# Two-tile attention units: queries, values, reciprocals and late transposes in another order

## Chip, cores and metric
The kernel runs on one core of a Trainium2 chip. The metric is the device time of one execution in microseconds (us); lower is better.

## What is computed
Four cross-attention layers in a row over x of shape (8, 256, 256), with one context ctx of shape (8, 64, 256) as keys and values; all in fp32. The change is within layers 0 and 2. Their core is, for each of the 8 batch rows:

```python
q = (layernorm(x) @ q_w + q_b)          # layer 0: x itself, context normalised
k, v = ctx @ k_w + k_b, ctx @ v_w + v_b  # 16 heads of 16
attn = softmax(where(mask, q k^T / 4, min))   # 256 x 64 per head
x = x + (attn v) @ w_o + bias            # layer 0: tanh(gate) * (...)
```

Layer 1 is the same with 32 heads of 8 and a layer norm after the sum. Layer 2 goes on with an MLP of 1024, and layer 3 is two attentions with heads of 128 and another MLP.

## The kernel before, in words
Five engines run their own instruction lists; semaphores tie them. Layers 0 to 2 are 24 units, one for each layer and batch row (`UNITS`, units 0 to 7, 8 to 15, 16 to 23; `NU` = 24). A unit of layer 0 or 2 has two tiles of 128 queries by 16 heads by 64 keys, one of layer 1 has four. Tiles are numbered through (`FIRST[u]` is the first of unit u).

The work is a pipeline over the units. In turn u TensorE makes the scores of unit u (`masks` L553, then `both_scores` L566 in two turns 0 and 1, two banks `sc`), the transposes of the last tile of unit u-1 (`late_tiles`, `probs_transposed` L588), the values of unit u+1 (`values` L477, bank work[3]), the source transposes of unit u+2 from unit 8 on (`source` L499, bank work[2]), the transposes of the softmax reciprocals of unit u-1 (`reciprocals_transposed` L597), the weighted values of u-1 (`weighted` L613, bank work[2]), the transposes of the first tile of unit u (banks work[0], work[1]), the queries of unit u+1 (`queries` L515, bank work[3]) and the output product of u-1 (`output` L633). A unit without a source product runs all but that.

VectorE reduces the maximum of each tile (L1112) and subtracts it (L1128), ScalarE takes the exponential (`exponentials`, L1631) and copies each result out of its bank: the transposed tile (`probs_out`, L1638), values (L1602), queries (L1567 and L1570), source, reciprocals (`reciprocals_out`, L1655). GpSimd adds the exponentials in halves and quarters (L1948, L1951), VectorE finishes the sum (L1134) and takes the reciprocal (L1141), and GpSimd spreads it over the head's columns (L1938); those go to TensorE to be transposed. VectorE's list has `unit_residual(u-2)`, the late tile's sum, `unit_reciprocals(u-1)` and only then the maximum of unit u's first tile. In layer 0's unit 5 VectorE also splits a bias in parts (`bias_parted`, L1168). In unit 17 ScalarE's `ln_finish` (L1616) and GpSimd's `norm_affine` (L1968) finish layer 1's last row. Layer 1's units have an order of their own in the same loops (`len(tiles) == 4`), and unit 16 too (`len(late) == 2`).

Of the kernel before, what the change touches and what calls it, by code (L numbers as in the profile page):

```python
# [98 lines left out]
def build(nc, A, out):  # L99
    with ExitStack() as ctx:  # L100
# [248 lines left out]
        def spread_done(u):  # L349
# [3 lines left out]
            return (a_spr, n) if u + 1 < NU and UNITS[u + 1][0] == 1 else (p_spr, u + 1 - n)  # L353

        def mlp_bank(b):

            return work[3] if b == 0 else work[2 + b % 2]
# [82 lines left out]
        def tensor(e):  # L440
# [74 lines left out]
            def queries(u):  # L515
                layer, _ = UNITS[u]
                w = w_small[f"l{layer}_wq"]
                e.wait_ge(s_in[f"l{layer}_wq"], 16)
                if u < B:
                    e.wait_ge(s_in["xT0" if u < 2 else "xT1"], 16)  # L520
                    src = xT[:, u, :, :]
                else:
                    e.wait_ge(a_sT, u - B + 1)
                    src = srcT[u % 3]


                if u > 0:
                    e.wait_ge(a_vd, u + 1)
                if u < 2 or 1 not in (UNITS[u - 1][0], UNITS[u - 2][0]):
                    e.wait_ge(a_rT, u - 1)  # L530
                if UNITS[u] == (1, 6):
                    e.wait_ge(a_key, 6)
                for o in range(DC):
                    for c in range(DC):
                        last = mm(work[3][:, o * T:(o + 1) * T], w[:, c, o * P:(o + 1) * P], src[:, c, :],  # L535
                                  start=(c == 0), stop=(c == DC - 1))
                last.then_inc(pe_q, 1)
# [50 lines left out]
            def probs_transposed(k):  # L588
                e.wait_ge(a_exp, k + 1)
                for half in range(2):  # L590
                    e.wait_ge(a_pT, 2 * (k - 1) + half + 1)
# [5 lines left out]
            def reciprocals_transposed(u):  # L597

                e.wait_ge(*spread_done(u))

                e.wait_ge(a_vd, min(u + 3, NU))
                e.wait_ge(a_qT, min(u + 2, NU))
                if u + 1 < NU and 1 in (UNITS[u][0], UNITS[u + 1][0]):
                    e.wait_ge(a_qT, u + 3)
                if u == NU - 1:
                    e.wait_ge(d_mT, 2)
                for c in range(DC):
                    for t in range(TT):
                        last = tr(work[3][:, c * T + t * P:c * T + (t + 1) * P], spread[u % 2][:, t, c * P:(c + 1) * P],
                                  ident[:, :])  # L610
                last.then_inc(pe_rT, 1)
# [58 lines left out]
            def mlp_source(b):  # L670
                e.wait_ge(*NORMS["m2", b])
                if b == 0:

                    e.wait_ge(a_rT, NU - 1)
                elif b == 1:
                    e.wait_ge(a_rT, NU)
                elif b == 2:
                    e.wait_ge(d_res, NU)
                else:
                    e.wait_ge(d_mT, 2 * (b - 2) + 2)  # L680
# [18 lines left out]
            def projected(b):  # L699
# [4 lines left out]
                if b < 2:  # L704
                    e.wait_ge(a_pT, 2 * NK)
                else:
                    e.wait_ge(d_mr, b - 1)
# [17 lines left out]
            for u in range(NU + 1):  # L725
# [35 lines left out]
                else:  # L761
                    if u + 1 < NU:
                        values(u + 1)
                        both_scores(u, 1)
                    if B <= u + 2 < NU:
                        source(u + 2)
                    for k in late:
                        probs_transposed(k)
                    if u == NU - 1:
                        both_scores(u, 1)  # L770
                    if u == NU:
                        hidden(0, 0)
                    if u > 0:
                        reciprocals_transposed(u - 1)
                        weighted(u - 1)
                    if u == NU:
                        hidden(0, 1)
                if tiles:
                    probs_transposed(tiles[0])
                if u + 1 < NU and len(late) < 2:  # L780
                    queries(u + 1)
                if u == NU - 1:
# [760 lines left out]
        def scalar(e):  # L1543
# [108 lines left out]
            def reciprocals_out(u):  # L1652
                e.wait_ge(pe_rT, u + 1)
                e.wait_ge(d_o, u - 1)
                act(recT_bufs[u % 2], work[3][:, :], ACT.Copy).then_inc(a_rT, 1)  # L1655

# [31 lines left out]
            for u in range(NU + 1):  # L1688
# [31 lines left out]
                if len(late) == 2:  # L1720
# [4 lines left out]
                    unit_source(u + 2)  # L1725
                    unit_queries(u + 1)
                else:
                    if u + 1 < NU:
                        unit_values(u + 1)
                    if B <= u + 2 < NU:  # L1730
                        unit_source(u + 2)
                    if u == NU:
                        mlp_source_high(0)
                    for k in late:
                        probs_out(k)
                    if tiles:
                        exponentials(tiles[0])
                if u > 0:
                    reciprocals_out(u - 1)
                if ended[0] == 1:  # L1740
                    ln_finish(("l1", ended[1]), xb(ended[1]), xb(ended[1]))
                if tiles:
                    probs_out(tiles[0])
                    exponentials(tiles[1])
                if u + 1 < NU and len(late) < 2:
                    unit_queries(u + 1)
                if u + 2 < NU and UNITS[u + 2][0] == 1:
# [425 lines left out]
```

## Time and profile before

| | us |
|---|---|
| median of 3 runs | 1095.81 |
| lowest, highest | 1095.37, 1098.17 |
| the profiled execution | 1095.92 |
| its span | 1094.0 |
| TensorE busy | 1008.7 (92%) |
| VectorE, ScalarE, GpSimd busy | 650.5, 512.8, 401.1 |

The span runs from the first to the last instruction. PE is TensorE, DVE VectorE, ACT ScalarE, POOL GpSimd. The chain of work that ended last lies on PE for 78% of the span, on ACT for 8%, POOL 5%, DVE 4%. The units of layers 0 to 2 end at about 368 us; the rest is the two MLPs and layer 3.

### The profile page before, as it was taken

The numbers are of one execution on the slowest core, as the hardware profiler recorded it, in microseconds if no ns is written. First come the engines' busy times: TensorE is split into PE (matmuls) and PEld (weight loads), VectorE is DVE, ScalarE is ACT, GpSimd is POOL, SyncE is SP. The second block draws the span as 40 slices with busy tenths as digits, with TensorE's granted clock in tenths as the row PEclk, the third lists the DMA queues.
The fourth block names the chain that finished last, engine by engine and source line by source line (L and its number), as shares of the span: only waits on it lengthen the run. The fifth ranks groups of instructions, "written<-read, shape, count | busy, mean of one in ns | idle before, by whom it ended". The sixth has DMA issues, their size and how long they took to land.

```text
span 1094.0 us, 18102 instructions
## 1 busy us (share of the span) xinstructions
PE 1008.7 (92%) x7252; PEld 794.6 (73%) x7252; DVE 650.5 (59%) x1119; ACT 512.8 (47%) x1026; POOL 401.1 (37%) x424
## 2 busy tenths in 40 slices
PE   5988888888789799899999999999999999989997
PEld 3656555545566699887777777777777777759997
DVE  4558887787678568735444555775345444465552
ACT  2446776675677545434323332333233323345542
POOL 2433578768976433201112212321122122253110
PEclk9999998999999999999999999999999999999999
DMA  9102000000000150020000022310000000200000
GB/s 329 44 2 78 1 1 1 1 1 1 1 2 1 44 208 1 1 78 1 1 1 1 1 75 81 116 39 1 1 1 1 1 1 1 77 1 11 20 20 30
DMA packets 17463, 34.90 MB, mean 32 GB/s; under 512 B 3554, under 2 KB 8420, under 8 KB 16740
## 3 DMA queue, kind: packets, MB, share of 16 engines
q1 hardware_dynamic: 17380, 33.75, 8.9%
q8 instruction: 57, 0.93, 0.3%
q14 instruction: 26, 0.21, 0.1%
HBM read 31.65 MB, written 2.10 MB: 31 GB/s over the span
## 4 chain that ended last, share of the span: by engine, by line
PE 78%; ACT 8%; POOL 5%; DVE 4%; issue 3%; DMA 0%; SPq 0%; POOLq 0%; ACTq 0%; DVEq 0%
PE work L928 11%; PE work L805 10%; PE scores L864 10%; PE work L881 5%; PE work L917 4%; PE work L593 3%; PE work L535 3%; PE work L645 3%; PE work L666 3%; PE work L667 3%; PE work L668 3%; PE scores L666 3%; PE scores L668 3%; PE scores L667 3%; PE work L447 2%
## 5 line engine op out<-in xcount | busy, mean ns | idle before, releaser
L928 PE MATMUL work<-pair,probsT 128*128 128x256 f32 x512 | 118.8, 385 | 11.1 <-ACT pair L1821 8.9
L1907 POOL TENSOR_SCALAR stat<-stat 128x2 f32<-128x2 f32 (+1 forms) x49 | 11.1, 227 | 298.8 <-DVE stat L1050 297.4
L928 PEld LDWEIGHTS work<-pair,probsT 128*128 128x128 f32 x512 | 94.6, 190 | 34.9 <-issue 20.4
L805 PE MATMUL work<-ctxT,w 128*128 128x128 f32 x992 | 116.1, 275 | 1.8 <-ACT pair L1821 1.1
L805 PEld LDWEIGHTS work<-ctxT,w 128*128 128x128 f32 x992 | 114.5, 192 | 3.0 <-ACT pair L1821 1.3
L864 PE MATMUL scores<-pair,act_bufs 128*128 128x512 f32 x256 | 115.2, 593 | 0.0
L1812 ACT ACTIVATE pair<-work 128x512 f32<-128x512 f32 x64 | 38.2, 597 | 160.3 <-PE work L881 160.3
L1802 ACT ACTIVATE kvT<-work,cols 128x128 f32<-128x128 f32 x120 | 34.2, 368 | 142.2 <-PE work L805 142.2
L2061 POOL TENSOR_TENSOR probs<-probs,smax 128x1024 f32<-128x1024 f32 x22 | 42.0, 1908 | 150.9 <-DVE smax L1439 150.9
L1419 DVE TENSOR_REDUCE smax<-scores 128x16 f32<-128x1024 f32 x32 | 39.2, 1224 | 79.6 <-PE scores L864 79.6
L864 PEld LDWEIGHTS scores<-pair,act_bufs 128*128 128x128 f32 x256 | 46.3, 190 | 46.0 <-issue 45.9
L881 PEld LDWEIGHTS work<-kvT,w 128*128 128x128 f32 x512 | 61.9, 192 | 15.3 <-issue 15.3
L1410 DVE TENSOR_TENSOR kvT<-work,cols 128x512 f32<-128x512 f32 x32 | 22.1, 691 | 83.8 <-PE work L805 83.8
L1112 DVE TENSOR_REDUCE smax<-scores 128x16 f32<-128x1024 f32 x48 | 58.3, 1214 | 16.7 <-PE scores L581 16.2
L881 PE MATMUL work<-kvT,w 128*128 128x128 f32 x512 | 62.4, 275 | 1.8 <-issue 1.8
L917 PE MATMUL work<-w,kvT 128*64 128x256 f32 x512 | 62.3, 385 | 0.0
L593 PE MATMUL work<-ident,pair 128*128 128x128 f32 x256 | 36.7, 289 | 24.9 <-ACT w L1638 12.9
L593 PEld LDWEIGHTS work<-ident,pair 128*128 128x128 f32 x256 | 29.4, 147 | 41.3 <-ACT pair L1631 36.1
L1948 POOL TENSOR_TENSOR pair<-pair 128x512 f32<-128x512 f32 x32 | 41.2, 1289 | 32.8 <-ACT pair L1631 32.2
L1960 POOL TENSOR_TENSOR x<-x,rows_late 128x512 f32<-128x512 f32 x32 | 47.8, 1497 | 10.3 <-DVE act_bufs L1056 8.6
L1638 ACT ACTIVATE w<-work 128x512 f32<-128x512 f32 x88 | 47.5, 592 | 8.2 <-PE work L593 8.1
L1948 POOL TENSOR_TENSOR pair<-probs 128x512 f32<-128x512 f32 x32 | 40.9, 1277 | 27.9 <-ACT probs L1631 27.7
(190 smaller groups left out, 2577.0 us busy)
## 6 DMA issues: line engine op xcount, KB each, us to landing
w<-in_l_wk SPq DMA_DIRECT2D x8, 512.0 KB, 6.1
w<-in_l_wq SPq DMA_DIRECT2D x8, 512.0 KB, 6.7
w<-in_l_wo SPq DMA_DIRECT2D x8, 512.0 KB, 7.6
w<-in_l_wv SPq DMA_DIRECT2D x8, 512.0 KB, 5.2
x<-in_x SPq DMA_DIRECT2D x1, 2048.0 KB, 13.0
out<-x SPq DMA_DIRECT2D x8, 256.0 KB, 2.1
pair<-in_xT SPq DMA_DIRECT2D x1, 1536.0 KB, 7.3
pair<-in_l_fc SPq DMA_DIRECT2D x1, 1024.0 KB, 4.9
```

Of the source, the lines that this page charges most:

```text
L593: last = tr(work[half][:, q * P:(q + 1) * P], probs[k % 4][:, (4 * half + q) * P:(4 * half + q + 1) * P], ident[:, :])
L666: mm(bank, s_hi, m_hi, start=start, stop=False)
L667: mm(bank, s_hi, m_lo, start=False, stop=False)
L668: return mm(bank, s_lo, m_hi, start=False, stop=stop)
L805: last = mm(bank[:, h * P:(h + 1) * P], w[:, c, (4 * g + h) * K3:(4 * g + h + 1) * K3], ctxT[:, c, p * P:(p + 1) * P], start=(c == 0), sto ...
L864: last = mm(sc[j % 2][:, half * BANK:(half + 1) * BANK], fixed[j // 2 % 2][:, c, t * P:(t + 1) * P], pk[n % 2][:, bb, c, half * BANK:(half ...
L881: last = mm(step_banks(j)[2 + c][:, h * P:(h + 1) * P], w3_wq[:, 4 * g + h, c * P:(c + 1) * P], kvT[i % 2][:, h, :], start=True, stop=True)
L917: last = mm(bank[h * S:(h + 1) * S, bb * D:(bb + 1) * D], kvT[2][:, 2 * q + h, bb * S:(bb + 1) * S], w3_wo[:, 4 * g + 2 * q + h, :], start ...
L928: last = mm(step_banks(j + 1)[0][:, 0:D], probsT_bufs[j % 2][:, q, :], pv[n % 2][:, bb, q, :], start=(q == 0), stop=(q == GH // 2 - 1))
L1112: v.tensor_reduce(smax[k % 2][:, 0:GH], s3, X, ALU.max).then_inc(d_max, 1)
L1948: g.tensor_tensor(halves, e3[:, :, 0:n], e3[:, :, n:S], ALU.add).then_inc(p_half, 1)
L1960: g.tensor_tensor(xb(b), xb(b), row(name).unsqueeze(1).broadcast_to([P, TT, D]), ALU.add).then_inc(done, 1)
```

## The change
In the turns of two-tile units, other than unit 16's, TensorE's list is reordered. Before: scores turn 0, values, scores turn 1, source, late tile's transposes, reciprocals' transposes, weighted values, first tile's transposes, queries, output. After: scores turn 0, late tile's transposes, scores turn 1, source, reciprocals' transposes, values, weighted values, queries, first tile's transposes, output. ScalarE's list follows: late tile's copies, source, reciprocals, values, first exponential, queries, (normalisation), first tile's copies, second exponential. Before it was values, source, late tile's copies, first exponential, reciprocals, (normalisation), first tile's copies, second exponential, queries. Between two-tile units the reciprocals' transposes write work[0] (`reciprocals_bank`), whose next use waits for their copy. In unit 0 the values stay ahead of the second turn. The waits are those that the new banks and order need. The lists of VectorE, GpSimd and the DMA queue stay.

```diff
+        def in_pairs(u):
+            return u > 0 and UNITS[u - 1][0] != 1 and (u == NU or UNITS[u][0] != 1)
+        def reciprocals_bank(u):
+            return work[0] if in_pairs(u + 1) else work[3]
@@ queries
                 if u > 0:
                     e.wait_ge(a_vd, u + 1)
-                if u < 2 or 1 not in (UNITS[u - 1][0], UNITS[u - 2][0]):
-                    e.wait_ge(a_rT, u - 1)
@@ probs_transposed
                 e.wait_ge(a_exp, k + 1)
+                u = UNIT_OF[k]
+                if k == FIRST[u] and in_pairs(u):
+                    e.wait_ge(a_rT, u)
@@ reciprocals_transposed
                 e.wait_ge(*spread_done(u))
-                e.wait_ge(a_vd, min(u + 3, NU))
-                e.wait_ge(a_qT, min(u + 2, NU))
-                if u + 1 < NU and 1 in (UNITS[u][0], UNITS[u + 1][0]):
+                if in_pairs(u + 1):
+                    e.wait_ge(a_pT, 2 * FIRST[u + 1] - 1)
+                else:
+                    e.wait_ge(a_vd, u + 3)
                     e.wait_ge(a_qT, u + 3)
@@ TensorE, two-tile units
-                    if u + 1 < NU:
+                    for k in late:
+                        probs_transposed(k)
+                    if u == 0:
                         values(u + 1)
+                    if tiles:
                         both_scores(u, 1)
                     if B <= u + 2 < NU:
                         source(u + 2)
-                    for k in late:
-                        probs_transposed(k)
-                    if u == NU - 1:
-                        both_scores(u, 1)
                     if u == NU:
                         hidden(0, 0)
                     if u > 0:
                         reciprocals_transposed(u - 1)
+                        if u + 1 < NU:
+                            values(u + 1)
                         weighted(u - 1)
                     if u == NU:
                         hidden(0, 1)
+                    if u + 1 < NU:
+                        queries(u + 1)
                 if tiles:
                     probs_transposed(tiles[0])
-                if u + 1 < NU and len(late) < 2:
-                    queries(u + 1)
@@ ScalarE
-                act(recT_bufs[u % 2], work[3][:, :], ACT.Copy).then_inc(a_rT, 1)
+                act(recT_bufs[u % 2], reciprocals_bank(u)[:, :], ACT.Copy).then_inc(a_rT, 1)
@@ ScalarE, two-tile units
+                    reciprocals_out(u - 1)
+                else:
                     if u == NU:
                         mlp_source_high(0)
                     for k in late:
                         probs_out(k)
+                    if B <= u + 2 < NU:
+                        unit_source(u + 2)
+                    if u > 0:
+                        reciprocals_out(u - 1)
+                    if u + 1 < NU:
+                        unit_values(u + 1)
                     if tiles:
                         exponentials(tiles[0])
-                if u > 0:
-                    reciprocals_out(u - 1)
+                    if u + 1 < NU:
+                        unit_queries(u + 1)
                 if ended[0] == 1:
                     ln_finish(("l1", ended[1]), xb(ended[1]), xb(ended[1]))
                 if tiles:
                     probs_out(tiles[0])
                     exponentials(tiles[1])
-                if u + 1 < NU and len(late) < 2:
-                    unit_queries(u + 1)
```

The first sources of the MLP and its projections wait for other counts of the same copies (`mlp_source`, `projected`).

## Rows read from the trace of the kernel before

**Rows 1.** Windows, stages of two-tile units: length, busy per engine, clock, DMA, GB/s
```profile
18.20:113.20 95.00, 82.51 (x754) 57.92 (x752) 59.55 (x77) 51.30 (x94) 40.88 (x48) 0.98 0.20 69
...
267.20:368.30 101.10, 87.15 (x814) 64.20 (x815) 72.17 (x123) 67.19 (x125) 76.33 (x103) 0.97 0.01 1
```

**Rows 2.** Timeline, TensorE, unit 4: start, busy, line, out<-in, count, idle before
```profile
62.43 0.61 PE L562 MATMUL scores<-mask_l,ones_bf 64*128 64x512 bf16 x4
62.96 0.73 PE L581 MATMUL scores<-w,pair 32*128 32x128 f32 x16
63.62 1.08 PE L495 MATMUL work<-w,pair 128*64 128x256 f32 x8
64.63 0.73 PE L581 MATMUL scores<-w,pair 32*128 32x128 f32 x16
65.29 1.09 PE L593 MATMUL work<-ident,pair 128*128 128x128 f32 x8
66.22 0.60 PE L609 MATMUL work<-ident,pair 128*128 128x128 f32 x4
67.12 1.07 PE L629 MATMUL work<-w,pair 128*32 128x256 f32 x16 [0.30 <-ACT w L1638]
69.02 1.09 PE L593 MATMUL work<-ident,probs 128*128 128x128 f32 x8 [0.83 <-ACT probs L1631]
69.95 1.89 PE L535 MATMUL work<-pair,w 128*128 128x256 f32 x8
71.68 1.89 PE L645 MATMUL work<-w,pair 128*128 128x256 f32 x8
```

**Rows 3.** Timeline of the other engines, around the start of unit 4
```profile
60.34 1.06 ACT L1631 ACTIVATE pair<-pair 128x1024 f32<-128x1024 f32 x1 [0.61 <-DVE pair L1128]
...
65.98 1.08 ACT L1638 ACTIVATE w<-work 128x512 f32<-128x512 f32 x2 [0.61 <-PE work L593]
...
63.65 0.42 DVE L1134 TENSOR_REDUCE sums<-pair 128x16 f32<-128x256 f32 x1 [0.36 <-POOL pair L1951]
64.10 0.35 DVE L1141 RECIPROCAL recs<-sums 128x32 f32<-128x32 f32 x1
65.39 1.22 DVE L1112 TENSOR_REDUCE smax<-scores 128x16 f32<-128x1024 f32 x1 [0.94 <-PE scores L581]
...
61.53 1.27 POOL L1948 TENSOR_TENSOR pair<-pair 128x512 f32<-128x512 f32 x1 [1.40 <-ACT pair L1631]
62.89 0.73 POOL L1951 TENSOR_TENSOR pair<-pair 128x256 f32<-128x256 f32 x1
...
64.52 0.61 POOL L1938 COPY pair<-recs 128x512 f32<-128x512 f32 x1 [0.33 <-DVE recs L1141]
```

**Rows 4.** Timeline, the start (units 0 and 1) and unit 5 on VectorE
```profile
25.75 3.31 PE L535 MATMUL work<-pair,w 128*128 128x256 f32 x8
...
33.00 0.60 PE L609 MATMUL work<-ident,pair 128*128 128x128 f32 x4
...
30.66 0.61 POOL L1938 COPY pair<-recs 128x512 f32<-128x512 f32 x1 [0.34 <-DVE recs L1141]
...
88.10 0.90 DVE L1175 CAST bias_parts<-pair 1x256 bf16<-1x256 f32 x3
```

**Rows 5.** Timeline, layer 2: turns 17, 18, 23 (TensorE), 17 and 19 (the others)
```profile
293.76 0.65 PE L609 MATMUL work<-ident,pair 128*128 128x128 f32 x4 [2.06 <-POOL pair L1938]
...
305.40 0.66 PE L609 MATMUL work<-ident,pair 128*128 128x128 f32 x4 [0.84 <-POOL pair L1938]
...
363.57 1.62 PE L593 MATMUL work<-ident,pair 128*128 128x128 f32 x8 [2.07 <-ACT pair L1631]
...
295.62 1.08 ACT L1620 ACTIVATE x<-x,stat 128x256 f32<-128x256 f32 x2
...
322.79 0.82 ACT L1570 ACTIVATE pair<-work,cols 128x256 f32<-128x256 f32 x2
...
297.45 1.27 POOL L1970 TENSOR_TENSOR x<-x,pair 128x512 f32<-128x512 f32 x1
```

More of the change, by code:

```diff
@@ L599, in reciprocals_transposed @@
                 e.wait_ge(*spread_done(u))
-                e.wait_ge(a_vd, min(u + 3, NU))
-                e.wait_ge(a_qT, min(u + 2, NU))
-                if u + 1 < NU and 1 in (UNITS[u][0], UNITS[u + 1][0]):
+                if in_pairs(u + 1):
+                    e.wait_ge(a_pT, 2 * FIRST[u + 1] - 1)
+                else:
+                    e.wait_ge(a_vd, u + 3)
                     e.wait_ge(a_qT, u + 3)
-                if u == NU - 1:
-                    e.wait_ge(d_mT, 2)
                 for c in range(DC):
                     for t in range(TT):
-                        last = tr(work[3][:, c * T + t * P:c * T + (t + 1) * P], spread[u % 2][:, t, c * P:(c + 1) * P],
+                        last = tr(reciprocals_bank(u)[:, c * T + t * P:c * T + (t + 1) * P], spread[u % 2][:, t, c * P:(c + 1) * P],
                                   ident[:, :])
@@ L672, in mlp_source @@
                 if b == 0:
-                    e.wait_ge(a_rT, NU - 1)
-                elif b == 1:
-                    e.wait_ge(a_rT, NU)
+                    e.wait_ge(a_qT, NU)
                 elif b == 2:
                     e.wait_ge(d_res, NU)
+                elif b == 1:
+                    e.wait_ge(d_mT, 2)
                 else:
@@ L705, in projected @@
                     e.wait_ge(a_pT, 2 * NK)
+                    e.wait_ge(a_rT, NU)
                 else:
@@ L766, in tensor @@
                         source(u + 2)
-                    for k in late:
-                        probs_transposed(k)
-                    if u == NU - 1:
-                        both_scores(u, 1)
                     if u == NU:
@@ L1726, in scalar @@
                     unit_queries(u + 1)
+                    reciprocals_out(u - 1)
                 else:
[L1728 to L1731, printed above, removed]
                     if u == NU:
```

## Prediction
> **What bounds the kernel now.** I read the busy times by stage first. The two stages of two-tile units hold 95.0 us (eight units of layer 0) and 101.1 us (the handover from layer 1 and eight units of layer 2); TensorE is busy for 82.5 and 87.2 us of them at a granted clock of 0.98 and 0.97, so some 26 us of gaps are the most that the change can touch [rows 1]. The stages before, between and after keep their order. Then I read TensorE's timeline of one steady unit [rows 2]. Its scores start at 62.43 and the next unit's 11.07 later (each start moves by that from unit to unit). Only two waits stand in it: 0.30 us before the weighted values (L629) and 0.83 us before the first tile's transposes (L593), both for ScalarE. The loop through the second is: scores, maximum and subtraction (VectorE), exponential (ScalarE), transposes, queries, output, the next scores. Last I read the other engines between two units, because the change moves work across that wait [rows 3]. There runs a second loop, hidden now: last exponential of the unit (60.34), two partial sums on GpSimd (61.53, 62.89), sum and reciprocal on VectorE (63.65, 64.10), spread on GpSimd (64.52, ends 65.13), then the reciprocals' transposes (L609). TensorE comes to those only at 66.22, so 1.04 us of slack hides that chain.
>
> **The change, part by part.** (a) The queries (1.73 us from start to start) go ahead of the first tile's transposes, and the late tile's transposes and then the reciprocals' transposes go ahead of the values. The work is the same, TensorE has 9.9 us of it in a unit. If nothing were late, the 1.13 us would go from every unit. (b) On ScalarE the copy of the queries goes ahead of the copies of the first tile's transposes and of the second tile's exponential. (c) The values now wait in TensorE's queue behind the reciprocals' transposes, and the weighted values, the queries, the first tile's transposes and the output behind them. (d) The bank is another (work0 instead of work3): the added wait is for half a tile's copy, long done; I cost it at nothing, it is hidden by (c), and at most the 0.5 us of one copy if it weren't. No DMA and no arithmetic is added; SP's queue is not moved.
>
> What is late next is the second loop. I put the start of the reciprocals' transposes at R. Transposes 0.58, values 1.01, weighted values 1.00, queries 1.73 [rows 2]: the first tile's transposes start at R+4.32 (its exponential is done by R+3.3). ScalarE starts to copy them 0.69 after their start (65.29 to 65.98), two copies take 1.0, so the second exponential starts at R+6.02. From its start to a usable spread it is 60.34 to 65.13 and a hop of 0.05: 4.84 [rows 3]. The period is 6.02 + 4.84 = 10.86 us against 11.07. TensorE would reach the reciprocals 2.8 us into a unit and waits there until 3.8: a 1.0 us wait takes the place of 1.13. A steady unit of layer 0 gains 0.2 us, not 1.1. In layer 2 the copy of the queries is 0.82 instead of 0.58 us [rows 5], so 11.1: no gain, and 0.03 lost.
>
> (e) Start. The first spread ends at 31.27, while TensorE gets to it at 33.00, behind queries that ran slowly after a gap, 3.31 instead of 1.89 us [rows 4, 2]. Now the queries fill that gap: gain 1.7. Three units at 0.2 make it 2.3. At the fifth, the keys of layer 1 on TensorE cover the spread, so its stalls really go, 1.1 more; but behind it VectorE's bias parts (from 88.10, 4.6 us in all) hold the next unit, and start when the first tile's sum is in, 2.7 us earlier [rows 4]. From there 10.9 against some 11.5 us for the last unit: I get 3.0 us of lead at the first four-tile unit. Layer 1 waits for data only, so it should hand the lead on.
>
> (f) Turns 17 and 18, the first of layer 2 in the new order. At 293.76 TensorE has already waited 2.06 us for the spread, which GpSimd and VectorE set, not TensorE [rows 5]. That moment doesn't move, but 1.01 us of values now come after it. Worse, ScalarE's normalisation for layer 1 (at 295.62) stood behind the reciprocals' copy and now stands behind the queries' copy, which ends near 299.0; GpSimd's two affine steps (from 297.45, 1.3 us each) wait for it at the head of its queue, and behind them stand a variance step and the partial sums of the next unit. Step by step: normalised 300.1, affine 302.8, variance 304.4, partial sums 306.5, sum and reciprocal 307.3, spread 308.0 against 305.40 now: 2.6 us lost. 0.3 of it comes back by the next unit, the steady ones lose 0.1 more, and the last unit, whose maximum now waits for the reciprocals, loses 0.4: layer 2 loses 3.0.
>
> (g) TensorE's clock. At 363.57, after 2.07 us of gap, eight transposes took 1.62 us instead of 1.09 (I read that as time at the lower of the clock's two levels, 1.2 GHz), and at 25.75 the queries took 3.31; at 293.76, after 2.06 us, nothing slowed [rows 5, 4]. An episode costs about 1.5 us (3.31 - 1.89 = 1.4 on the queries alone). The change makes a gap of about 3.1 us ahead of 293.76 (0.9 and 2.06 lay apart before, with transposes between), which I take to cost 1.4, and splits the gap before 363.57 into two of 1.3, which I take to save 1.5.
>
> The sum: -3.0 + 3.0 + 1.4 - 1.5 = -0.1 us. The profiled execution took 1095.92 (span 1094.0, 1.9 around it), 0.1 above the median of 1095.81. The sum gives 1095.8 on it; the small errors (0.1 in a period, some eleven times) lean neither way, and I round to 1096.0.
>
> The Trainium skill, "Perfetto Trace Analysis", Identifying the Most-Contended Engine, says to optimise the engine with the highest occupancy first. TensorE is that engine by the rows and its waits are what the change goes for; taken so, the gain would be rival 1's. The same page's section Matmul Optimizations says that the engine scales its power with utilisation and matmuls should come back to back; the slowed rows at 25.75 and 363.57 agree, and it speaks against a change that collects gaps in one place (rival 2).
>
> **Rivals.**
> 1. TensorE becomes the bound, because the spread isn't late. Then 14 units lose 1.13 us and the start 1.7: 17.5, giving 1078. Against it: the chain of 4.84 us is measured, and none of its links is shortened. It would need the second exponential 1.0 us earlier than I have it. Chance 0.07.
> 2. Slower by TensorE's clock: the wait before the reciprocals' transposes of turn 1 (2.0 us by my working) and those of turns 17 and 18 (3.1 and 1.9) each end in the lower level, and the one near 363.57 isn't avoided: -3.0 + 3.0 + 3 x 1.5 = +4.5, giving 1100.4. For it: gaps of 2.07 did it. Against: 2.06 didn't. It decides from a second episode on. Chance 0.18.
> 3. Layer 1 doesn't hand on the lead (its units are set by GpSimd, VectorE and ScalarE in turn, and ScalarE's lead is only 2.4): up to +3.0 on my sum, 1099. Chance 0.1.
> 4. The first units of layer 2 don't lose, because GpSimd catches up: -3.0 - 1.5 and a rest of +0.5, giving 1092. For it: GpSimd has free time in later units. Against: its queue is full from 284 to 305. Chance 0.14.
> 5. The change does nothing: the order is as written but every wait reappears in place. 1095.8. Against: the start's queries have nothing to wait for. Chance 0.03.
> My forecast: 0.48.
>
> **How the numbers follow.** A measurement of this kernel can tell about 0.3% (3.3 us) from no change. Faster by more (under 1092.5): rival 1, most of rival 4 and a tail of the forecast, 0.25. Slower by more (over 1099.1): most of rival 2, half of rival 3 and a tail of the forecast, 0.24. Same: 0.51. The forecast's own range is 1092.5 to 1099.5; with rivals 2 to 4 it is 1090.5 to 1100.8, which leaves out rival 1 and the far ends of the others.
>
> **What would show it.** Right: a wait of about 1.0 us for GpSimd before L609's counterpart in every steady unit, none before the first tile's transposes, a period of 10.9 us in layer 0 and 11.1 in layer 2; the scores of the first four-tile unit 3 us earlier; GpSimd's affine step of the last layer-1 unit after the queries' copy; the reciprocals' transposes of turn 18 at least 2.6 us later, counted from the scores of turn 17. Wrong: periods near 9.9, or no wait for GpSimd. The prediction fails most easily at the clock, whose episodes I can only bound, and at the handover.

## The result, and the profile after

The changed kernel takes 1105.81 us (median of 4 runs, 1104.33 to 1108.47) against 1096.99 us for the kernel before beside it (1095.37 to 1099.27): a ratio of 1.0087, interval 1.0067 to 1.0107. It is slower by 9 us. The forecast of no change, 1096.0 with a range to 1100.8, was wrong. The profiled execution of the changed kernel has a span of 1104.0 us, 10.0 more than before. Ratios go by the fast executions alone, which leaves out one of all those below, of `layer1_filled`: 1485.48 us at a mean granted clock of 0.655.

Where the 10.0 us are, read from the starts of each turn's scores in TensorE's timeline (turn 16's first to turn 17's first, and so on; "first product" is that of the MLP):

| stretch, us | before | after | difference |
|---|---|---|---|
| start to the first scores | 18.2 | 17.8 | -0.4 |
| turns 0 to 7 | 95.0 | 93.6 | -1.4 |
| turns 8 to 15 (layer 1) | 154.0 | 155.5 | +1.5 |
| turn 16 | 19.3 | 19.6 | +0.3 |
| turns 17 and 18 | 26.2 | 34.1 | +7.9 |
| turns 19 to 22 | 44.3 | 45.2 | +0.9 |
| turn 23 to the first product | 13.0 | 12.6 | -0.3 |
| the rest | 724.1 | 725.7 | +1.6 |

The steady turns went as forecast. TensorE's timeline of turn 4 of the changed kernel (start, busy, line, out<-in, count, idle time before it and who ended it), the counterpart of [rows 2]:

```profile
59.98 0.61 PE L566 MATMUL scores<-mask_l,ones_bf 64*128 64x512 bf16 x4
60.51 0.73 PE L585 MATMUL scores<-w,pair 32*128 32x128 f32 x16
61.17 1.09 PE L601 MATMUL work<-ident,pair 128*128 128x128 f32 x8
62.19 0.73 PE L585 MATMUL scores<-w,pair 32*128 32x128 f32 x16
63.80 0.66 PE L617 MATMUL work<-ident,pair 128*128 128x128 f32 x4 [0.88 <-POOL pair L1949]
64.38 1.08 PE L502 MATMUL work<-w,pair 128*64 128x256 f32 x8
65.40 1.07 PE L637 MATMUL work<-w,pair 128*32 128x256 f32 x16
66.40 1.99 PE L539 MATMUL work<-pair,w 128*128 128x256 f32 x8
68.23 1.04 PE L601 MATMUL work<-ident,probs 128*128 128x128 f32 x8
69.10 1.89 PE L653 MATMUL work<-w,pair 128*128 128x256 f32 x8
```

The waits for ScalarE before the weighted values (L637) and before the first tile's transposes (L601) are gone. In their place stands one of 0.88 us before the reciprocals' transposes (L617), for GpSimd's spread. Turns 2 and 3 take 10.95 us from scores to scores (49.03 to 59.98), against 11.07. Turn 4 holds the keys of layer 1 as well: its next scores come 16.36 us later, before 16.48 (62.43 to 78.91). The other engines around the start of the turn before it, the counterpart of [rows 3]:

```profile
47.98 1.07 ACT L1641 ACTIVATE probs<-probs 128x1024 f32<-128x1024 f32 x1
...
51.31 0.42 DVE L1144 TENSOR_REDUCE sums<-pair 128x16 f32<-128x256 f32 x1 [1.42 <-POOL pair L1962]
51.76 0.35 DVE L1151 RECIPROCAL recs<-sums 128x32 f32<-128x32 f32 x1
52.03 1.20 DVE L1122 TENSOR_REDUCE smax<-scores 128x16 f32<-128x1024 f32 x1
...
49.19 1.27 POOL L1959 TENSOR_TENSOR pair<-probs 128x512 f32<-128x512 f32 x1 [1.77 <-ACT probs L1641]
50.54 0.74 POOL L1962 TENSOR_TENSOR pair<-pair 128x256 f32<-128x256 f32 x1
...
52.18 0.61 POOL L1949 COPY pair<-recs 128x512 f32<-128x512 f32 x1 [0.33 <-DVE recs L1151]
```

The chain is the same as before, link by link: exponential 47.98, partial sums 49.19 and 50.54, sum 51.31, reciprocal 51.76, spread from 52.18 to 52.79. TensorE takes it up at 52.85 now; before, it came 1.09 us after the spread's end. VectorE's next maximum stands behind the reciprocal in the same list and isn't held up by it: it starts at 52.03, just behind the end of its scores (51.24 and 0.73).

The large loss is in turns 17 and 18. TensorE, ScalarE and GpSimd there:

```profile
293.74 1.12 PE L617 MATMUL work<-ident,pair 128*128 128x128 f32 x4 [2.92 <-POOL pair L1949]
294.79 1.98 PE L502 MATMUL work<-w,ctxT 128*64 128x256 f32 x8
296.69 1.94 PE L637 MATMUL work<-w,pair 128*32 128x256 f32 x16
298.56 2.36 PE L539 MATMUL work<-act_bufs,w 128*128 128x256 f32 x8
...
308.47 0.63 PE L454 MATMUL work<-ident,act_bufs 128*128 128x128 f32 x4 [1.98 <-ACT act_bufs L1630]
310.79 1.12 PE L617 MATMUL work<-ident,pair 128*128 128x128 f32 x4 [1.70 <-POOL pair L1949]
311.84 1.98 PE L502 MATMUL work<-w,ctxT 128*64 128x256 f32 x8
...
301.68 1.09 ACT L1630 ACTIVATE x<-x,stat 128x256 f32<-128x256 f32 x2
...
302.85 1.27 POOL L1981 TENSOR_TENSOR x<-x,pair 128x512 f32<-128x512 f32 x1 [2.24 <-ACT x L1630]
```

TensorE stands still for 2.92 us before 293.74, and the values and weighted values that follow take 1.98 and 1.94 us instead of 1.08 and 1.07; the same again after 310.79, where gaps of 1.98 and 1.70 us lie ahead. In the windows over the two stretches the last column but two is the granted clock: 0.50, the lower of the two levels (1.2 GHz of 2.4), in both.

```profile
293.70:297.00 3.30, 3.26 (x16) 1.69 (x20) 2.41 (x6) 0.79 (x2) 1.22 (x1) 0.50 0.00 0
310.70:314.00 3.30, 3.21 (x16) 1.70 (x20) 3.27 (x7) 0.75 (x3) 1.26 (x2) 0.50 0.02 7
```

### The profile page after: what moved, and what is told of

Read it like the earlier page. It is cut to its first block, busy times and chain, and to the rows that moved or that the text cites. A ratio compares the mean times of both kernels' runs of the same rounds, so it can differ in the third digit from the quotient of the medians.

```text
span 1104.0 us, 18116 instructions
## 1 busy us (share of the span) xinstructions
PE 1019.5 (92%) x7252; PEld 799.0 (72%) x7252; DVE 652.5 (59%) x1119; ACT 512.7 (46%) x1026; POOL 402.4 (36%) x424
## 4 chain that ended last, share of the span: by engine, by line
PE 75%; ACT 9%; POOL 8%; issue 4%; DVE 3%; DMA 0%; POOLq 0%; SPq 0%; ACTq 0%; DVEq 0%
PE work L938 11%; PE work L815 10%; PE scores L874 10%; PE work L891 5%; PE work L927 4%; PE work L539 3%; PE work L674 3%; PE work L676 3%; PE work L675 3%; PE scores L674 3%; PE scores L676 3%; PE scores L675 3%; POOL pair L1959 3%; PE work L637 2%; PE work L601 2%
## 5 line engine op out<-in xcount | busy, mean ns | idle before, releaser
L1918 POOL TENSOR_SCALAR stat<-stat 128x2 f32<-128x2 f32 (+1 forms) x49 | 11.2, 228 | 299.3 <-DVE stat L1060 297.9
L601 PE MATMUL work<-ident,pair 128*128 128x128 f32 x256 | 38.3, 298 | 20.2 <-ACT w L1648 11.9
L1144 DVE TENSOR_REDUCE sums<-pair 128x16 f32<-128x256 f32 x64 | 26.4, 412 | 51.4 <-POOL pair L1962 51.1
L601 PEld LDWEIGHTS work<-ident,pair 128*128 128x128 f32 x256 | 31.1, 152 | 34.5 <-ACT pair L1641 28.4
## 6 DMA issues: line engine op xcount, KB each, us to landing
x<-in_x SPq DMA_DIRECT2D x1, 2048.0 KB, 12.6
```

The costliest lines, as they stand in the source:

```text
L601: last = tr(work[half][:, q * P:(q + 1) * P], probs[k % 4][:, (4 * half + q) * P:(4 * half + q + 1) * P], ident[:, :])
```

## Experiments

All kernels below were compared with the kernel before on the same chip. Theory: in the new order the chain of exponential, sums, reciprocal and spread bounds a turn, and what is lost comes from turns 17 and 18, part by GpSimd's queue and part by TensorE's clock. Rivals: the queries' new place bounds; the loss is the clock's alone; it is the new order's everywhere.

**One layer at a time.** `first_layer_only` has the new order in turns 0 to 7, `third_layer_only` in turns 17 to 24:

```diff
+        def new_order(u):
+            return u < 16          # the other kernel: u > 16
+
         def in_pairs(u):
-            return u > 0 and UNITS[u - 1][0] != 1 and (u == NU or UNITS[u][0] != 1)
+            return new_order(u) and u > 0 and UNITS[u - 1][0] != 1 and (u == NU or UNITS[u][0] != 1)
```

(Not shown: where `new_order` is false, each list has its order and waits of before.)

> The new order in turns 0 to 7 only, turns 17 to 24 as before. Theory (the chain of sums and spread on GpSimd and VectorE sets the period, and the loss is in layer 2): period 10.95 us in turns 1 to 4 as in the changed kernel, the first four-tile unit 1.4 to 1.8 us earlier than before, and the total between 1094 and 1097 against 1096 before, ratio 0.998 to 1.001. Rival (layer 1 swallows any lead): the same periods, but unit 16's scores where they were, within 0.3 us, and ratio 1.000 to 1.002. Second rival (the whole change hurts everywhere): ratio above 1.003.

Measured: 1097.79 us, ratio 0.9999 (0.9982 to 1.0017). The period is 10.96 to 10.97 us, turns 0 to 7 take 92.6 us (2.4 less than before, 1.0 less than in the changed kernel, whose turn 6 had a slowed stretch). But layer 1 took 155.7 us in the profile, 1.7 more than before, so unit 16's scores were 1.0 earlier in time and only 0.7 counted from the first scores. The ratio is the first theory's (the time is 0.8 us over its range; the kernel before beside it had 1097.08), but the first four-tile unit came 2.7 us earlier and not 1.4 to 1.8. The rival on the lost lead has a point, taken up below.

> The old order in turns 0 to 7, the new one in turns 17 to 24. Theory: the whole loss is here: 8 us between the scores of turn 17 and the MLP's first product, ratio 1.007 to 1.009, some 1104 to 1106 us. Rival (much of the loss comes from the shifted phase of the granted clock in layer 1, from the other part of the change): turn 17 to the MLP loses under 5 us, ratio under 1.005.

Measured: 1108.72 us, ratio 1.011 (1.0093 to 1.0126), above the theory's 1.009. From turn 17's scores to the first product it is 92.1 us against 83.5: 8.6 us lost, as the theory has it. The profiled span is 12.4 us longer than before. Of the other 3.8, layer 1 has 1.7 (155.7 us), turn 16 has 0.6 and the stretch behind the MLP's first product 1.6, with no instruction of these three moved. So most of the loss is layer 2's, the rival of a loss everywhere falls, and the part in layer 1 comes without any instruction up to there being moved.

**The clock in turns 17 and 18.** `clock_kept` fills TensorE's wait with transposes of the identity that nobody reads:

```diff
+                    for _ in range({17: 24, 18: 14}.get(u, 0)):
+                        tr(work[3][:, 0:P], ident[:, :], ident[:, :])
                     if u > 0:
                         reciprocals_transposed(u - 1)
```

> The changed kernel with idle transposes of the identity into a free bank (work3) ahead of the reciprocals' transposes: 24 in turn 17, 14 in turn 18. They change no result and fill the wait for the spread. Theory (clock and queue order each have a share): the granted clock stays at 1.0 after both waits, values and weighted values take 1.0 us each again instead of 1.9, turns 17 and 18 are 9 to 5 us shorter in sum by 2.6 us each at most, so 4 to 5 us in all: ratio to before 1.004 to 1.005. Rival 1 (the clock is all of the loss): ratio 1.000 to 1.002. Rival 2 (the lower clock costs nothing, since the next wait ends on GpSimd's queue): ratio stays 1.008 to 1.009.

Measured: 1101.0 us, ratio 1.0044 (1.0029 to 1.0059). TensorE's timeline of that kernel, with the fill in L812, and its windows:

```profile
293.05 2.78 PE L812 MATMUL work<-ident 128*128 128x128 f32 x24
296.14 0.66 PE L626 MATMUL work<-ident,pair 128*128 128x128 f32 x4 [0.31 <-POOL pair L1998]
296.73 1.08 PE L505 MATMUL work<-w,ctxT 128*64 128x256 f32 x8
297.74 1.07 PE L646 MATMUL work<-w,pair 128*32 128x256 f32 x16
...
308.87 3.19 PE L812 MATMUL work<-ident 128*128 128x128 f32 x14
```

```profile
293.70:297.00 3.30, 2.99 (x27) 2.51 (x27) 3.23 (x6) 0.78 (x3) 3.18 (x6) 1.00 0.00 0
308.00:312.00 4.00, 3.71 (x19) 3.74 (x20) 2.86 (x4) 2.54 (x6) 3.38 (x5) 0.58 0.02 4
```

At 296.73 and 297.74 values and weighted values take 1.08 and 1.07 us at a clock of 1.00. In turn 18 the fill itself (308.87) ran at the lower level, after a gap of 1.98 us before the source, and ended late. Turns 17 and 18 take 30.2 us instead of 34.1: the clock had a share of 3.9 us at least, and 4.0 us remain against 26.2, so the clock alone doesn't explain the loss.

The same profile shows a third such place, the first of those that rival 2 of the prediction names. Before the reciprocals' transposes of turn 1 TensorE waits 2.00 us in the new order. Behind it the values took 1.51 and the weighted values 1.94 us here (31.63, 33.07), and turn 1 took 13.9 us, as in the profile of `ln_first_filled`; in those of the changed kernel, of `first_layer_only` and of `ln_first` both ran at full pace, and turn 1 took 12.3 to 12.4.

**GpSimd's queue in turn 17.** `ln_first` lets ScalarE normalise layer 1's last row ahead of the queries' copy:

```diff
                     if tiles:
                         exponentials(tiles[0])
+                    if ended[0] == 1:
+                        ln_finish(("l1", ended[1]), xb(ended[1]), xb(ended[1]))
                     if u + 1 < NU:
                         unit_queries(u + 1)
```

(Not shown: the call further down is skipped in that turn.)

> The changed kernel with one move on ScalarE in turn 17: the normalisation of layer 1's last row ahead of the copy of the queries, instead of behind it. Theory (part of the loss is GpSimd's queue: its two affine steps wait for this normalisation and hold the next spread): the normalisation starts near 298.3 instead of 301.7, the affine steps start when the partial sums end (300.6 instead of 302.9), and the reciprocals' transposes of turn 18 come 2.2 us earlier, ratio to before 1.006 to 1.007. Rival (the clock alone): turn 18 stays where it was, ratio 1.008 or more.

Measured: 1100.57 us, ratio 1.0035 (1.0021 to 1.0049), more of a gain than expected. The normalisation and the first affine step in this kernel's timeline:

```profile
296.88 1.08 ACT L1662 ACTIVATE x<-x,stat 128x256 f32<-128x256 f32 x2
...
299.19 1.27 POOL L2030 TENSOR_TENSOR x<-x,pair 128x512 f32<-128x512 f32 x1
```

Turn 17's first scores start at 285.23 in that profile, so the affine step comes 14.0 us into the turn, against 16.4 in the changed kernel (302.85 - 286.43). The reciprocals' transposes of turn 18 come 21.9 us in (307.15) against 24.4 (310.79 - 286.43), and 19.0 before (305.40 in [rows 5], turn 17's scores at 286.44). Turns 17 and 18 take 31.9 us, 2.2 less than the 34.1, so GpSimd's queue has this share. The loss is neither the clock's alone nor the queue's. The ratio fell by more than these 2.2 us account for. The profile of `ln_first` also lacks the slowed stretch in turn 6 (13.1 us against 14.1) and that in layer 1 (154.0 against 155.5), which the edit doesn't touch; how often either comes was not measured.

**Both.** `ln_first_filled` joins the two edits.

> The changed kernel with both: the normalisation ahead of the queries' copy in turn 17, and the idle transposes (24 and 14) ahead of the reciprocals' transposes in turns 17 and 18. From the scores of turn 17 to those of turn 19 it was 26.2 us before, 34.1 changed, 30.2 with the fill alone and 31.9 with the move alone. Theory (two separate causes that add, GpSimd's queue 2.2 us and the clock 3.9 us): 28.0 us, and a ratio to before of 1.000 to 1.002. Rival (they overlap: the fill only helped because the later wait was long): 29.5 us or more, ratio 1.003 or more.

Measured: 27.9 us for turns 17 and 18, what two causes that add would leave: 34.1, less 3.9 for the clock and 2.2 for the queue, is 28.0. 1.7 us remain against 26.2; of what they consist was not tried (the 1.01 us of values that now stand behind each wait are my reading). But the time is 1099.95 us, the ratio 1.0032 (1.0017 to 1.0047), no better than `ln_first` alone and in the range that I had given the rival; the turns decide for the theory, the ratio doesn't. Between the two profiles the 4.0 us gained in turns 17 and 18 (27.9 against 31.9) stand against 1.6 lost in turn 1 (13.9 against 12.3) and 1.7 in layer 1 (155.7 against 154.0), two stretches that both edits leave as they were. Turns 19 to 22 (45.4 us against 44.3 before) and the wait before the MLP's first product (1.70 against 0.55) are long in both; they are taken up below. How much each holds over all executions stays open.

**The chain's length.** A GpSimd instruction of 0.7 us that nobody reads stands ahead of each spread, in the kernel before, the changed kernel and the one of the next paragraph:

```diff
                 e.wait_ge(pe_rT, u - 1)
+                e.wait_ge(p_spare, spares)
+                g.tensor_tensor(spare[:, :], ones[:, 0:2], minus_half[:, 0:2], ALU.pow).then_inc(p_spare, 1)
                 for i in range(n):
```

(Not shown: the lines that count `spares` and a wait for the constants.)

> The kernel before with one more GpSimd instruction of 0.7 us (a power on a spare 128x2 tile) ahead of each spread of the two-tile units, some 0.8 us in the chain. Theory: 1.04 us of slack hide it, the period in turns 2 to 4 stays 11.07 us. Rival (GpSimd's chain bounds the kernel before as well): 11.8 us.

> The changed kernel with the same extra 0.7 us GpSimd instruction ahead of each spread. Theory (the chain bounds it): the period in turns 2 to 4 grows from 10.95 by all of it, to 11.7 to 11.8 us, and TensorE's wait before the reciprocals' transposes from 0.88 to 1.7. Rival (the late queries' copy and second exponential bound, the spread is only near): under 11.3 us.

Measured in the profiles: 11.07 and 11.08 us a turn before, unchanged; 11.63 and 11.65 in the changed kernel, 0.69 more than 10.95: all of the instruction, which takes 0.71. Turns 19 to 22 say the same: 44.3 us before, with the instruction or without; 47.9 against 45.2 in the changed kernel. (Each ran once, for its profile: 1100.79 and 1115.04 us.) The reciprocals' transposes of turn 3, first in the changed kernel with the longer chain (whole wait 1.56 us, was 0.88), then in turn 4 of the kernel before with it (no wait):

```profile
56.84 0.65 PE L628 MATMUL work<-ident,pair 128*128 128x128 f32 x4 [1.56 <-POOL pair L2003]
```

```profile
65.84 0.60 PE L611 MATMUL work<-ident,pair 128*128 128x128 f32 x4
```

The same 0.7 us is free in one and paid in full in the other: the bound changed hands. Had the queries' new place set the period without the spread, the changed kernel would not have felt it, so that rival falls. But the loop that binds runs through the queries too. Once round it in the changed kernel: the reciprocals' transposes at 52.85, values, weighted values and queries, the first tile's transposes at 57.28, the second exponential at 58.93, the chain of sums and spread, the reciprocals' transposes at 63.80. That is 4.43, 1.65 and 4.87 us, the 10.95 of the period.

**Taking the wait off the path.** Only VectorE's product before the output needs the reciprocals. `recips_behind_weighted` puts their transposes behind the weighted values:

```diff
                     if u > 0:
-                        reciprocals_transposed(u - 1)
                         if u + 1 < NU:
                             values(u + 1)
                         weighted(u - 1)
+                        reciprocals_transposed(u - 1)
@@ ScalarE
-                    if u > 0:
-                        reciprocals_out(u - 1)
                     if u + 1 < NU:
                         unit_values(u + 1)
+                    if u > 0:
+                        reciprocals_out(u - 1)
```

(`weighted` of unit 4 gets a wait for the bias on its bank, which the spread had implied.)

> The changed kernel with the reciprocals' transposes moved behind the values and the weighted values (and their copy behind the values' copy on ScalarE); nothing between them needs the reciprocals. Theory (the wait for the spread is the bound, 1.0 us before the reciprocals' transposes in each steady unit): the 2.0 us of values and weighted values cover it, the period falls to 9.9 to 10.1 in layer 0 and 10.4 to 10.7 in layer 2, 7 us gained by the first four-tile unit and 3 or more in layer 2: 1084 to 1091 us, ratio 0.990 to 0.996. Rival (the queries ahead of the first tile's transposes are what bounds, by the later second exponential): period stays at 10.9 and ratio above 1.004.

Measured: 1090.38 us, ratio 0.995 (0.9931 to 0.9969), faster than the kernel before and the changed one. Turn 4 on TensorE:

```profile
55.88 0.61 PE L571 MATMUL scores<-mask_l,ones_bf 64*128 64x512 bf16 x4
...
58.76 1.08 PE L505 MATMUL work<-w,pair 128*64 128x256 f32 x8
59.77 1.07 PE L648 MATMUL work<-w,pair 128*32 128x256 f32 x16
60.77 0.66 PE L626 MATMUL work<-ident,pair 128*128 128x128 f32 x4
61.27 1.89 PE L544 MATMUL work<-pair,w 128*128 128x256 f32 x8
63.06 1.09 PE L606 MATMUL work<-ident,probs 128*128 128x128 f32 x8
63.99 1.89 PE L664 MATMUL work<-w,pair 128*128 128x256 f32 x8
```

No wait is left; the period is 9.92 to 9.94 us, the 9.9 of TensorE's own work, and with the queries still ahead of the first tile's transposes. From the reciprocals' transposes to the first tile's it is now 2.29 us (60.77 to 63.06) instead of 4.43, so the loop would be 8.8 us by estimate (2.29 + 1.65 + 4.87), and TensorE's own work is longer. The gain is all ahead of layer 1: its first scores come at 104.62, 8.6 us earlier than before, and unit 16's at 258.59, the same 8.6. In layer 2 the expectation missed: 11.4 us a turn (11.7 in turn 21) instead of 10.4 to 10.7, since the weighted values wait 0.7 us for ScalarE's copy of the source there, and from turn 17 to the MLP's first product it took 84.6 us where it was 83.5 before: 1.1 lost, not 3 gained. With the longer chain:

> The reciprocals' transposes behind the weighted values everywhere, with the extra 0.7 us GpSimd instruction ahead of each spread. Theory: the spread comes near 4.5 us into a turn and TensorE needs it near 4.9, so the period in turns 2 to 4 stays at 9.9 to 10.0 us. Rival (the chain is at its limit there too): 10.6 us.

Measured: 9.93 us in turns 2 to 4 (the whole took 1098.51 us in one run, lost in later stages that I didn't follow). The cover is there.

**A better mix.** `moved_first_layer` is that order in turns 0 to 7 and 22 to 24 and the order of before in 17 to 21 (`new_order` is `u < 16 or u > 21`).

> The new order with the reciprocals' transposes behind the weighted values in turns 0 to 7 and 22 to 24, and the order of before in turns 17 to 21, where the moved form had periods of 11.4 us against 11.1. Theory: period 9.93 in layer 0, 11.08 in turns 19 to 21, 10.4 in turn 22; 8 us ahead at unit 16 less up to 1.6 us for the clock in layer 1, and 1 us more than the moved form over all: 1087 to 1091 us, ratio 0.992 to 0.996, at or below recips_behind_weighted. Rival (the lead is lost at the handover to layer 2, whose first units are set by GpSimd): ratio above 0.997.

Measured: 1091.81 us, ratio 0.9939 (0.9919 to 0.9958); the ratio is in the expected range, the time 0.8 us above it. The interval overlaps that of the form before it; the two are not told apart.

**The 1.6 us of layer 1.** Layer 1 took 154.0 us in some profiles and 155.5 to 155.7 in others, with and without a lead: 154.0 before and with the 8.6 us of lead above, 155.7 in `third_layer_only` and 155.6 in `longer_chain_before`, which have the order of before up to there. The first transposes behind a gap of 2.38 us took 1.06 us in three turns of the kernel before (at 165.07, 185.09, 205.05). The same three in the changed kernel, same gap:

```profile
163.27 1.94 PE L601 MATMUL work<-ident,pair 128*128 128x128 f32 x8 [2.38 <-ACT w L1648]
183.04 1.73 PE L601 MATMUL work<-ident,pair 128*128 128x128 f32 x8 [2.38 <-ACT probsT L1648]
203.04 1.27 PE L601 MATMUL work<-ident,pair 128*128 128x128 f32 x8 [2.38 <-ACT w L1648]
```

`layer1_filled` is the kernel before with 18 idle transposes in that gap, in the turns from 9 on:

```diff
                     scores(*tiles_of(u)[0])
+                    if 9 <= u:
+                        e.wait_ge(a_qT, u + 1)
+                        e.wait_ge(a_vd, u + 1)
+                        e.wait_ge(a_rT, u - 1)
+                        for _ in range(18):
+                            tr(work[3][:, 0:P], ident[:, :], ident[:, :])
                     probs_transposed(late[0])
```

> The kernel before with 18 idle transposes of the identity into work3 in each four-tile turn from turn 9 on, in the 2.4 us gap ahead of the first late tile's transposes. Theory (layer 1 takes 154.0 us when its gaps cost no clock, as in two of the profiles, and 155.5 to 155.7 when one or more do, as in four others, whatever the change): it takes 154.0 us from the first four-tile scores to unit 16's, no transposes of that group take over 1.2 us, ratio 0.998 to 1.000. Rival (the fill delays the transposes behind it, or the 1.6 us come from elsewhere): 155 us or more, ratio 1.001 or more.

Measured: 1094.81 us, ratio 0.9979 (0.9965 to 0.9993), and layer 1 took 152.3 us, less than the 154.0 that I took for undisturbed. Nine of its ten executions lie between 1093.2 and 1095.7 us, where the 23 of the kernel before lie between 1092.7 and 1099.3. The windows say why: two of the kernel before, in layer 1, then the same two filled.

```profile
165.00:170.00 5.00, 4.93 (x21) 3.78 (x23) 3.99 (x5) 2.44 (x4) 4.77 (x6) 0.66 0.01 3
185.00:190.00 5.00, 4.91 (x21) 3.62 (x23) 3.96 (x5) 2.45 (x4) 4.76 (x6) 0.66 0.01 3
```

```profile
165.00:170.00 5.00, 4.73 (x31) 3.42 (x31) 3.34 (x4) 2.58 (x6) 4.84 (x5) 1.00 0.00 0
185.00:190.00 5.00, 5.00 (x32) 3.18 (x30) 4.62 (x6) 2.86 (x6) 4.84 (x5) 1.00 0.00 0
```

Even the profile of before ran a part of each of these two stretches at the lower level (0.66 on average), only later than the first instruction behind the gap. So the gap costs in the kernel before too, and whether the drop meets the first instruction behind it differs from execution to execution.

`moved_and_filled` has this fill on `moved_first_layer`, and 16 more idle transposes ahead of the first tile's transposes of turn 23.

> moved_first_layer with idle transposes in two places: 18 in each four-tile turn from turn 9 on, 16 ahead of the first tile's transposes of turn 23. Theory: up to 1.6 us less in layer 1 and 1.5 us less in turn 23 against moved_first_layer: 1086 to 1090 us, ratio 0.990 to 0.994. Rival (idle work on TensorE delays more than the clock gives back): ratio 0.995 or more.

Measured: 1087.31 us (1085.96 to 1088.11), ratio 0.9913 (0.9891 to 0.9935). Layer 1 takes 152.3 us again. It is the fastest of all, 10.2 us under the kernel before beside it (1097.46). In turn 23 the fill gave back 0.5 us of the 1.5 expected (12.6 from its scores to the MLP's first product, against 13.1).

## Why the prediction was wrong

Point by point, by its own steps.

- The bound in a steady turn, (a) to (c): right. The wait is 0.88 us where I had 1.0, the period 10.95 where I had 10.86 and 11.07 was. What TensorE got back in layer 0, 1.13 us a turn, went into the wait for the spread but for 0.12. `longer_chain_before` and `longer_chain_after` show it. Of my three terms 4.43 us from the reciprocals' to the first tile's transposes was forecast as 4.32, 1.65 as 1.70 and 4.87 as 4.84. One reading was off: I gave turn 4 as a steady one, but the next unit's scores are 16.48 us behind its own; the 11.07 is that of turns 2, 3 and 5.
- (d) the other bank: no wait for it anywhere in the trace, as said.
- (e) the lead at the first four-tile unit: 3.0 forecast, 1.8 measured (its scores at 111.42 against 113.22), 2.7 in `first_layer_only` (110.48). Of both, 0.4 lies ahead of the first scores, where nothing was moved, so the change made 1.4 and 2.4. The 0.6 that even `first_layer_only` lacks is in part the period of 10.95 for 10.86; the other 1.0 is a slowed stretch in turn 6 of the changed kernel, after a gap of 1.67 us, which was not in the sum. But only 0.3 of the 1.8 was left at turn 16 (266.88 against 267.19).
- (f) the handover: right in mechanism. The reciprocals' transposes of turn 18 came 24.4 us after turn 17's scores, against 19.0 before: 5.4 us later where my working gave 2.6. Part of the excess is the clock of turn 17: in `clock_kept` it was 23.1 us, behind a fill that itself ended late. With the normalisation moved as well it was 20.8. Without the clock and the queue 1.7 us remain. (The terms as I gave them, 2.6 - 0.3 + 0.1 + 0.4, make 2.8; I wrote 3.0.)
- (g) the clock is the term that was mis-sized, and the step that failed. I priced one episode at 1.4 us, from queries that ran slow at the start [rows 4]. Behind the wait for the spread now stood all of values, weighted values and queries: turn 17 took 9.7 us from its reciprocals' transposes to the next scores where the undisturbed order takes 7.1, so 2.6 us an episode. And there were two, in turns 17 and 18, where I counted one. `clock_kept` gives 3.9 us for both, at least, since its fill in turn 18 was itself slowed; turn 17 alone went from 17.0 to 14.5 us. The 1.5 us that I credited for a gap split in two in turn 23 did not come either: its transposes ran at full clock (1.09 us), but the MLP's first product then waited 1.70 us instead of 0.55 for operands that VectorE and ScalarE had yet to make: the last of them (VectorE, `m_src_low`) ended at 378.25 and the product started at 378.35, before 369.83 and 369.93. Taking a cost off one engine gains nothing if another engine is next.
- Turns 19 to 22: 0.1 forecast, 0.9 measured. Turns 19 and 22 take 11.2 us instead of 11.09, what I had given the copy of the queries and a little more; turns 20 and 21 take 11.39 and 11.40. There GpSimd's power step took 1.24 us (at 318.04, 330.52 and 341.90) where it took 0.73 before, and the partial sums of the next tile follow in its queue without a wait. The step in turn 20, the partial sums behind it, VectorE's `m_w_low` at that moment (it splits a weight of the MLP), then the step and `m_w_low` in the kernel before:

```profile
341.90 1.24 POOL L1921 TENSOR_TENSOR stat<-stat,minus_half 128x2 f32<-128x2 f32 x1
343.70 1.29 POOL L1959 TENSOR_TENSOR pair<-probs 128x512 f32<-128x512 f32 x1
...
341.88 0.68 DVE L1214 TENSOR_TENSOR m_w_low<-pair,m_w_high 128x512 fp32r<-128x512 f32 x1
```

```profile
332.89 0.73 POOL L1910 TENSOR_TENSOR stat<-stat,minus_half 128x2 f32<-128x2 f32 x1
...
333.12 0.68 DVE L1204 TENSOR_TENSOR m_w_low<-pair,m_w_high 128x512 fp32r<-128x512 f32 x1
```

So 4 x 0.12 and 2 x 0.19 make the 0.9. That this queue is full there, and that a step in it can get longer, was not among my terms. The traces tell the two cases apart by which engine starts first. The traces have 24 steps of 1.24 us, three in each of the eight kernels with the new order in turns 19 to 21, and in all of them `m_w_low` had started 0.02 to 0.03 us ahead of the step. In the six with the order of before there, `m_w_low` started some 0.23 us behind the step, and each took its usual time. No other power step began while `m_w_low` ran. No run moved either instruction by itself, so this is a reading without exception and not a tested cause.
- Rivals: the second (slower by the clock, 1100.4, chance 0.18) names the main term but was sized at 1.5 us an episode. The third (layer 1 doesn't hand on the lead, chance 0.1) fits the 0.3 us left of the lead, but not by its reason: `recips_behind_weighted` handed on all of its 8.6 us, and the 1.5 that layer 1 lost in the changed kernel it also lost where nothing ahead of it was moved. I had let the rivals stand as alternatives, and the range ended at the worse of the two alone.
- The last 1.6 us of the table are the clock once more, in layer 3, where nothing was moved. Behind the same gap the same product took 1.7 us longer in the changed kernel, first row, than before, second row. The granted clock from 970 to 974 us was 0.72; around the product of the kernel before it was 1.00:

```profile
971.58 5.38 PE L938 MATMUL work<-pair,probsT 128*128 128x256 f32 x16 [2.35 <-ACT pair L1832]
```

```profile
963.21 3.69 PE L928 MATMUL work<-pair,probsT 128*128 128x256 f32 x16 [2.34 <-ACT pair L1821]
```

By stretch, of the 10.0 us between my sum (1095.8) and the profiled 1105.8: turns 17 and 18 cost 7.9 where I had 4.0 (2.6 and 1.4), so 3.9; the lead of turns 0 to 7 was short by 1.6; layer 1 has 1.5 and turn 16 has 0.3 that I had at nothing; turns 19 to 22 have 0.8; turn 23 gained 0.3 for 1.1; the rest has 1.6; and 0.4 ahead of the first scores goes the other way. The clock's part in this is at least 2.5 in turns 17 and 18 (3.9 for 1.4), 1.0 in turn 6, 1.5 in layer 1 and 1.6 in layer 3. The last two are hardly the change's own: the 5.38 us of layer 3 stand in seven of the fourteen profiles, `longer_chain_before` among them, and are absent from `ln_first_filled` and `longer_chain_after`; layer 1's 1.5 come and go in the same way.

## What to carry to other kernels

Before a wait is taken off the busiest engine, follow the loops that run beside it, and add up each one as it will be in the new order: what stands between a late result and the next step of its chain counts in full. Here the loop through the spread was some 8.5 us in the order before (an estimate: 66.22 to 69.02 in [rows 2] less the wait of 0.83, then 1.70 and 4.84), under the 11.07 of the turn. Values and queries set into it made it 10.95, and 1.13 us of waits became a gain of 0.12. With the values and weighted values ahead of the wait it was 8.8, and the turn fell to the 9.9 of TensorE's own work. When a consumer must wait, put it behind work that doesn't need it, and ask who truly needs the result: the reciprocals were wanted only at the output, and moving the values and weighted values ahead of them gave what the larger reordering did not. A gap gathered in one place on TensorE can cost twice: itself, and the work behind it at half the clock, as much as stands in the dependent chain there. And one profile on each side is not enough where the clock differs between executions: some 3 us of the 10.0 between these two lie in stretches that the change leaves alone.

## What the runs showed of the hardware

TensorE's granted clock fell after gaps shorter than the 2.07 us of [rows 5], and not each time: after 1.67 us in turn 6 of the changed kernel but not in `first_layer_only`, and after the 2.38 us of layer 1 with 1.06 us for the transposes behind it before and 1.27 to 1.94 us after. In the kernel before such drops were there too, unseen in the first instruction's time: behind the gap that ends at 165.07 the clock was 1.00 up to 166 us and 0.50 from there to 169. After 2.34 us of gap in layer 3 sixteen products took 3.69 us in one profile and 5.38 in another. Idle transposes of the identity, 0.12 us each, kept the clock at 1.00 (24 in a gap of 2.9 us, 18 in one of 2.4 us) and cost nothing where they ended before the awaited data. Behind a gap of 1.98 us fourteen of them ran slowed themselves, 3.19 us in all, in `clock_kept`; behind one of 1.04 us, in `ln_first_filled`, they took 1.69. GpSimd's power over a 128x2 tile took some 0.73 us in most places, and 1.24 in the 24 where VectorE's `m_w_low` (two 128x512 operands, 0.68 us) had started just before it; started 0.23 us behind it, the same `m_w_low` cost it nothing.
